# Row numbers selected with matmuls, and gathered tiles moved to dense targets 5, 9, 12, 16, 19 in a three-layer graph kernel

## The reference

```python
def _tagconv(x, src, dst, norm, W, b):          # K = 3
    out = x @ W[0]
    h = x
    for k in range(1, K + 1):
        msg = norm[:, None] * h[src]
        h = jax.ops.segment_sum(msg, dst, num_segments=x.shape[0])
        out = out + h @ W[k]
    return out + b

deg = segment_sum(ones, dst)
dis = where(deg > 0, rsqrt(maximum(deg, 1.0)), 0.0);  norm = dis[src] * dis[dst]
h = relu(_tagconv(x, src, dst, norm, W1, b1))
h = relu(_tagconv(h, src, dst, norm, W2, b2))
return layernorm(x + _tagconv(h, src, dst, norm, W3, b3))
```

## Time and profile before

| what | value |
|---|---|
| time before, median of 3 | 1302.9 us |
| the profiled execution's own time | 1303.25 us |
| its span, first to last instruction | 1301.5 us |
| TensorE busy in the span | 1249.0 us, 96% |
| GpSimd busy | 817.2 us, 63% |
| mean granted clock of TensorE | 0.994 |

### The profile page before, as it was taken

How to read it: one execution, slowest core, us unless ns; L and a number is a source line. 1 busy time by engine, 2 the same in 40 slices (tenths; PEclk the granted TensorE clock), 3 DMA queues, 4 the chain that set the end, 5 groups by cost and what they waited for, 6 DMA issues and landing times.

```text
span 1301.5 us, 19817 instructions
## 1 busy us (share of the span) xinstructions
PE 1249.0 (96%) x7584; PEld 631.7 (49%) x7584; DVE 636.8 (49%) x1621; ACT 359.5 (28%) x863; POOL 817.2 (63%) x914
## 2 busy tenths in 40 slices
PE   3789999999999999999999999999999999999996
PEld 2455555444455555444544455555444544454443
DVE  5886664344444556434443434455433433345654
ACT  3676665121112223111221112223111111112221
POOL 7347565566756572767566756573567566756673
PEclk9999999899999999999999999999999999999998
DMA  3433333344433342444354433342344344434553
GB/s 87 132 111 109 95 98 101 110 137 125 130 93 112 102 121 65 130 121 134 106 145 126 134 97 102 105 128 77 109 122 133 112 118 121 130 112 139 149 156 89
DMA packets 86967, 150.43 MB, mean 116 GB/s; under 512 B 19097, under 2 KB 60753, under 8 KB 86866
## 3 DMA queue, kind: packets, MB, share of 16 engines
q0 software_dynamic: 39184, 107.00, 29.4%
q1 hardware_dynamic: 47682, 42.10, 10.1%
HBM read 116.91 MB, written 32.11 MB: 115 GB/s over the span
## 4 chain that ended last, share of the span: by engine, by line
PE 86%; POOL 6%; issue 3%; DVE 2%; DMA 1%; ACT 1%; SPq 0%; POOLq 0%; ACTq 0%; DVEq 0%
PE pb L1093 64%; PE pb L1005 9%; POOL GB L782 4%; PE pb L1007 4%; PE pb L1024 4%; PE pb L931 2%; PE pb L1098 1%; PE pb L1071 1%; PE pb L1043 1%; DMA xr<-in_x 1%; DMA GB<-vh,KS 1%; POOL gT L696 0%; POOL g L766 0%; DVE pb L1437 0%; DVE V L1408 0%
## 5 line engine op out<-in xcount | busy, mean ns | idle before, releaser
L782 POOL DMA_INDIRECT GB<-vh,KS x810 | 779.3, 962 | 433.4 <-issue 235.5
L1093 PE MATMUL pb<-V,A 128*128 128x512 f16 x4104 | 936.7, 380 | 0.0
L1093 PEld LDWEIGHTS pb<-V,A 128*128 128x128 fp8e4 x4104 | 397.0, 98 | 442.3 <-issue 2.5
L1437 DVE SCALAR_TENSOR_TENSOR pb<-pb,cst,t 128x256 f32<-128x256 f32 (+1 forms) x225 | 110.0, 489 | 359.3 <-ACT t L896 359.2
L896 ACT ACTIVATE t<-pb,cst 128x256 f32<-128x256 f32 (+1 forms) x250 | 118.3, 473 | 500.6 <-PE pb L1098 429.3
L1005 PE MATMUL pb<-Whl,gT 128*128 128x512 f16 x576 | 204.7, 383 | 2.9 <-DVE KD L1349 1.7
L1007 PE MATMUL pb<-Whl,gT 128*128 128x256 f16 x576 | 158.0, 274 | 0.0
L1408 DVE SCALAR_TENSOR_TENSOR V<-V,pb 128x256 f16<-128x256 f16 (+1 forms) x225 | 94.1, 420 | 93.6 <-ACT V L870 93.4
L870 ACT ACTIVATE V<-pb 128x256 f16<-128x256 f32 (+1 forms) x225 | 85.7, 383 | 132.8 <-DVE pb L1437 132.7
L1005 PEld LDWEIGHTS pb<-Whl,gT 128*128 128x128 f16 x576 | 56.5, 98 | 78.7 <-issue 22.0
L1303 DVE TENSOR_REDUCE stat<-V 128x1 f32<-128x256 f16 x225 | 91.2, 411 | 0.2
(11 more groups left out here) (209 smaller groups left out, 568.6 us busy)
## 6 DMA issues: line engine op xcount, KB each, us to landing
vh<-V SPq DMA_DIRECT2D x216, 128.0 KB, 2.0
GB<-vh,KS POOLq DMA_INDIRECT x810, 2.8
xr<-in_x SPq DMA_DIRECT2D x48, 128.0 KB, 2.8
out<-g SPq DMA_DIRECT2D x24, 128.0 KB, 1.9
xr<-in_W SPq DMA_DIRECT2D x16, 128.0 KB, 2.3
V<-in_W SPq DMA_DIRECT2D x2, 512.0 KB, 4.5
vh<-V SPq DMA_DIRECT2D x18, 32.0 KB, 1.9
bb<-in_b SPq DMA_DIRECT2D x3, 128.0 KB, 5.1
```

The costliest lines, as they stand in the source:

```text
L782: pool.indirect_dma_start(GB[:, slot, :], None, vh[vbuf[(L, k + 1)]][:, :], bass.IndirectOffsetOnAxis(ap=KS[:, p:p + 1], axis=0))\
L1093: mm = pe.matmul(acc[:, :], A8[:, a, t * P:(t + 1) * P], src[:, a, :], start=False, stop=(n == NT - 1), skip_group_check=True)
L1437: dve.scalar_tensor_tensor(hi, hi, cst[0:r, 1, t:t + 1], lt, ALU.mult, ALU.add).then_inc(S["s_d1"], 1)
```

## The change

It has three parts. In the setup, `rules` becomes f32 and shrinks from twelve columns to six, `mine` holds more of the selection, and the matmuls now sum constants and selected counts in place; ACT's copy of the counts clips at zero; GpSimd needs two dependent steps for the row numbers and four for `place`. Second, `want` and `onesf` are set before that chain and not behind it. Third, `FIRST`, `STEPS`, `LATER` and the switch `hop_over` change: gathered tiles stand behind dense targets with index 4, 8, 11, 15 and 18, and the short tile 24, index 19, is the last of each hop. In hop 0 only the last two entries change (18: 22 and 19: 25 become 18: 25).

```diff
-FIRST = {3: 2, 5: 5, 7: 7, 9: 10, 11: 12, 13: 15, 15: 17, 17: 20, 18: 22, 19: 25}
-STEPS = {5: 5, 9: 10, 12: 15, 15: 20, 19: 25}
+FIRST = {3: 2, 5: 5, 7: 7, 9: 10, 11: 12, 13: 15, 15: 17, 17: 20, 18: 25}
+STEPS = {4: 5, 8: 10, 11: 15, 15: 20, 18: 25}
-RULED = 28
+RULED = 25
-LATER = (0, 2, 5, 9, 10, 15)
+LATER = (0, 0, 1, 2, 5, 9, 15)
...
-            pool.memset(rules, 0.0).then_inc(S["s_pc"], 1)
             pool.wait_ge(S["s_idx"], 1)
...
+            pool.memset(mine, 0.0).then_inc(S["s_pc"], 1)
+            pool.memset(rules, 0.0).then_inc(S["s_pc"], 1)
+            pool.memset(onesf[:, :], 1.0).then_inc(S["s_cst"], 1)
...
+            for d, a, b in ((0, 1, 1), (1, GRAN, -GRAN), (2, 1, -1), (5, -GRAN * FULL, -1)):
+                pool.memset(by[:, d, :, GV - 1], float(a)).then_inc(S["s_pc"], 1)
+                pool.memset(by[:, d, :, GV], float(b)).then_inc(S["s_pc"], 1)
...
+            picked(to[:, 0], 0, NPAIR, PW)
+            picked(to[:, 1], 2, NPAIR, PW)
+            picked(to[:, 2, :, 0:GV - 1], 0, NPAIR, GV - 1)
+            picked(to[:, 2, :, GV + 1:PW], 1, NPAIR, GV - 1)
+            picked(mine[:, 2, NE:NR].unsqueeze(2), 3, NTB, 1)
+            picked(to[:, 3, :, GV - 1:GV], 0, NPAIR, 1, -float(GRAN))
+            picked(to[:, 3, :, GV:GV + 1], 1, NPAIR, 1, float(GRAN))
...
-            pool.wait_ge(S["s_cp5"], 3)
+            pool.wait_ge(S["s_cp5"], 2)
...
-            done5(pool.tensor_scalar(vals[:, :], per[:, 12:16], 0.0, 0.0, ALU.max, ALU.add))
-            done5(pool.tensor_scalar(two[:, 0:1], vals[:, 0:1], float(FULL), 0.0, ALU.add, ALU.add))
-            done5(pool.tensor_scalar(vals[:, 2:3], vals[:, 2:3], two[:, 0:1], 0.0, ALU.min, ALU.add))
-            done5(pool.tensor_scalar(two[:, 1:2], vals[:, 0:1], per[:, 0:1], per[:, 4:5], ALU.mult, ALU.add))
...
-            done5(pool.tensor_copy(idx[0:NR, QW:QW + 1], two[:, 4:5]))
+            done5(pool.tensor_scalar(mid[:, 0:1], per[:, 4:5], float(FULL), per[:, 5:6], ALU.add, ALU.min))
+            done5(pool.tensor_scalar(idx[0:NR, QW:QW + 1], mid[:, 0:1], per[:, 0:1], per[:, 6:7], ALU.mult, ALU.add))
...
-            done5(pool.tensor_scalar(per[:, 11:12], per[:, 11:12], float(JZ), 0.0, ALU.add, ALU.add))
-            done5(pool.tensor_scalar(two[:, 5:6], vals[:, 0:1], per[:, 5:6], per[:, 9:10], ALU.mult, ALU.add))
-            done5(pool.tensor_scalar(two[:, 6:7], vals[:, 1:2], per[:, 6:7], two[:, 5:6], ALU.mult, ALU.add))
-            done5(pool.tensor_scalar(two[:, 7:8], vals[:, 2:3], per[:, 7:8], two[:, 6:7], ALU.mult, ALU.add))
+            done5(pool.tensor_scalar(mid[:, 1:2], mid[:, 0:1], per[:, 1:2], per[:, 7:8], ALU.mult, ALU.add))
...
-            pool.memset(onesf[:, :], 1.0).then_inc(S["s_cst"], 1)
...
-            act.activation(found[:, :], bank[1][0:4 * NPAIR, 0:1], ACT.Copy).then_inc(S["s_cp5"], 1)
+            act.activation(found[:, :], bank[1][0:4 * NPAIR, 0:1], ACT.Relu).then_inc(S["s_cp5"], 1)
             act.wait_ge(S["s_gc"], 2)
-            act.activation(per[:, 0:12], bank[0][0:NR, 0:12], ACT.Copy).then_inc(S["s_cp5"], 1)
-            act.wait_ge(S["s_gc"], 3)
-            act.activation(per[:, 12:16], bank[2][0:NR, 0:4], ACT.Copy).then_inc(S["s_cp5"], 1)
+            act.activation(per[:, :], bank[0][0:NR, 0:8], ACT.Copy).then_inc(S["s_cp5"], 1)
...
-            for d in range(12):
-                mm = pe.matmul(bank[0][0:NR, d:d + 1], rules[:, d, :], ones16[0:1, 0:1], start=True, stop=True,
+            pe.wait_ge(S["s_cst"], 18)
+            for d in range(4):
+                pe.matmul(bank[0][0:NR, d:d + 1], rules[:, d, :], onesf[0:1, 0:1], start=True, stop=True,
...
             for j in range(4):
-                mm = pe.matmul(bank[2][0:NR, j:j + 1], mine[:, j, :], found[:, :], start=True, stop=True,
+                mm = pe.matmul(bank[0][0:NR, 4 + j:5 + j], mine[:, j, :], found[:, :], start=True, stop=(j < 2),
+                if j >= 2:
+                    mm = pe.matmul(bank[0][0:NR, 4 + j:5 + j], rules[:, 2 + j, :], onesf[0:1, 0:1], start=False,
...
-                hop_over = (k, t) == (0, NT - 2) if k < 3 else hop_over
+                hop_over = (k, t) == (0, NT - 1) if k < 3 else hop_over
```

More of the change, by code:

```diff
@@ L484, in bass_tag_gnn_layernorm @@
         found = sb("found", [4 * NPAIR, 1], F32)
-        per = sb("per", [NR, 16], F32)
-        vals = sb("vals", [NR, 4], F32)
-        two = sb("two", [NR, 8], F32)
+        per = sb("per", [NR, 8], F32)
+        mid = sb("mid", [NR, 2], F32)
         tk = sb("tk", [P, 5, NTB], F32)
@@ L535, in bass_tag_gnn_layernorm @@
         less = gb[0:1, 256:256 + 4 * NPAIR]
-        rules = gb[0:1, 2048:2048 + 12 * NR].rearrange("p (d r) -> p d r", r=NR)
+        rules = gb[0:1, 2048:2048 + 12 * NR].bitcast(F32).rearrange("p (d r) -> p d r", r=NR)
         place = gb[0:NR, 4096:4096 + 2 * P].bitcast(F32)
@@ L704, in _ @@
-            pool.memset(by[:, 2, :, GV - 1:GV + 1], 1.0).then_inc(S["s_pc"], 1)
-            pool.memset(rules[:, 3, NE:NR], 1.0).then_inc(S["s_pc"], 1)
+            to = mine[:, :, 0:NE].rearrange("p j (u m) -> p j u m", m=PW)
+            pool.wait_ge(S["s_pc"], 6)
+            for d, a, b in ((0, 1, 1), (1, GRAN, -GRAN), (2, 1, -1), (5, -GRAN * FULL, -1)):
+                pool.memset(by[:, d, :, GV - 1], float(a)).then_inc(S["s_pc"], 1)
+                pool.memset(by[:, d, :, GV], float(b)).then_inc(S["s_pc"], 1)
@@ L711, in _ @@
[L711 to L720, removed]
@@ L721, in _ @@
-            pool.affine_select(out=mine[:, 3, NE:NR], in_=mine[:, 3, NE:NR], compare_op=ALU.not_equal, fill=1.0,
-                               base=-NPAIR * 3, pattern=[[-1, NTB]], channel_multiplier=1).then_inc(S["s_pc"], 1)
+            pool.iota(rules[:, 3, 0:NE].rearrange("p (g v) -> p g v", v=GV), pattern=[[GH, NE // GV], [0, GV]],
+                      base=ND, **iota).then_inc(S["s_pc"], 1)
+            pool.iota(rules[:, 3, NE:NR], pattern=[[GD, NTB]], base=BT * GD, **iota).then_inc(S["s_pc"], 1)
@@ new lines, in picked @@
+            def picked(z, j, n, width, value=1.0):
+                pool.affine_select(out=z, in_=z, compare_op=ALU.not_equal, fill=value, base=-NPAIR * j,
+                                   pattern=[[-1, n], [0, width]], channel_multiplier=1).then_inc(S["s_pc"], 1)
+            picked(to[:, 0], 0, NPAIR, PW)
[3 more added lines that the diff above has]
+            picked(mine[:, 2, NE:NR].unsqueeze(2), 3, NTB, 1)
@@ L723, in _ @@
+            picked(to[:, 3, :, GV - 1:GV], 0, NPAIR, 1, -float(GRAN))
+            picked(to[:, 3, :, GV:GV + 1], 1, NPAIR, 1, float(GRAN))
             pool.iota(place, pattern=[[1, P]], base=0, **iota).then_inc(S["s_pc"], 1)
+            for n, many in enumerate((float(E), 0.0, 15.0, float(E))):
+                pool.memset(want[:, n:n + 1], many).then_inc(S["s_cst"], 1)
             pool.wait_ge(S["s_pc"], RULED + 1)
-            pool.wait_ge(S["s_cp5"], 3)
+            pool.wait_ge(S["s_cp5"], 2)
@@ L755, in _ @@
             pool.tensor_tensor(wf[0:NR, P:2 * P], wf[0:NR, P:2 * P], place, ALU.add).then_inc(S["s_k5"], 1)
-            pool.memset(want[:, 0:1], float(E)).then_inc(S["s_cst"], 1)
-            pool.memset(want[:, 1:2], 0.0).then_inc(S["s_cst"], 1)
-            pool.memset(want[:, 2:3], 15.0).then_inc(S["s_cst"], 1)
-            pool.memset(want[:, 3:4], float(E)).then_inc(S["s_cst"], 1)
-            pool.memset(onesf[:, :], 1.0).then_inc(S["s_cst"], 1)
             pool.wait_ge(S["s_cs"], 1)
```

17 lines of the change are left out of this document (4 added, 13 removed).

## The result

The changed kernel took 1309.57 us, median of 5 runs (1309.05 to 1312.21), against 1302.9, the median of the five runs before (1300.92 to 1304.74): a ratio of 1.006, 95% interval 1.0048 to 1.0071. It is slower by about 0.6%; predicted were 1307.3 us and a range of 1298.5 to 1311. The spans differ by +6.1 us, and three places make that up: setup -3.4, end of hop 0 +1.6, hops 3 and 6 +8.0 (the small rest, -0.1, lies behind hop 7's first gathered tile).

The account below looks back on a forecast made before the run. TensorE is busy 1049.1 of 1050.5 us in hops 1 to 8, so the setup holds the room. 1303.25 - 4.0 + 3.4 + 5.0 = 1307.65, less 0.35 for the profiled execution: 1307.3 us, range 1298.5 to 1311.

Parts of the forecast that it names:

- Setup: Up to the first hop: a shorter GpSimd chain and an earlier `cst` save 4.0 us (bounds 1.5 and 5.5).
- each costs as much as a wide one: Setup constants on GpSimd: upper bound of +1.5 us if every narrow select costs like a wide one; +0.7 was forecast.
- The other path, `cst`: Setup on ACT: the degree root comes near 28.8 and not 33.4 us, so `cst` is ready 4.6 us earlier.
- End of hop 0: The short tile follows the gather waits instead of filling them, and the lower clock lasts longer: +3.4 us (+3.1 to +5.7).
- Hops 3 and 6: First hops of a layer: TensorE waits for deferred pieces and gathers, 2.6 us a hop at most, +5.0 for both (0 to 9).
- The other hops and the kernel's end: Hops 1, 2, 4, 5, 7, 8 and the last stores: gathers stay in time, only the last store is smaller; 0.
- the clock falls at hops 3 and 6: Rival: waits there lower the clock, 2.3 us each, and hop 0's short tile may pay as much; 1311.9 us, chance 0.09.
- the deferred pieces are absorbed: Rival: in hops 3 and 6 ACT and DVE keep up and gathers are in time; 1302.3 us, no change, chance 0.28.
- the setup gives far more: Rival: setup gives 4.6 us, projections lose half their 8.7 us idle time, hops 3 and 6 cost nothing; 1297.3 us, chance 0.13.
- hop 0's end is no longer than before: Rival: hop 0 ends no later within itself, the ring having moved, which needs gather 78 earlier; 1303.9 us, chance 0.08.

Follow-up runs that it names:

- Bank 7: The changed kernel with dense target 0 of hops 3 and 6 accumulating in PSUM bank 7, not the bank the short tile just left: 1307.09 us, ratio 1.004.
- setup only: The changed kernel with the order of before put back (`FIRST`, `STEPS`, `LATER`, `hop_over`), its setup kept: 1300.05 us, ratio 0.9977.
- short tile back: The changed kernel with `FIRST` of before alone, so hop 0's short tile again stands between the last gather matmuls: 1307.89 us, ratio 1.0036.
- constants early: The kernel before with only `want` and `onesf` set ahead of GpSimd's chain for the row numbers: 1300.15 us, ratio 0.9984.
- later demand: The setup only kernel with hop 0's gathered tiles given out one behind nearly each dense target: 1294.95 us, ratio 0.9937.

## Why the prediction was right, and which terms were off

The direction and the mechanism were right: a gain in the setup, and an order that loses more at the end of hop 0 and at hops 3 and 6. The time was 2.3 us over the forecast, inside its own range. That it came so near is in part luck: the cost of hop 0's end was set 1.8 us too high and that of hops 3 and 6 3.0 us too low.

- *Setup, -4.0 predicted, -3.4 in the trace (-2.4 by the medians).* Right in size, off in its steps. The seven selects took 2.22 us, 0.32 on average, where three had taken 0.95: the bound "each costs as much as a wide one" came nearest, and the constants came at 20.47 and not 19.6. The fetch was 0.5 us later than forecast. And behind it GpSimd's steps of 128 columns became slower, 0.97, 0.96 and two casts of 0.78 and 0.73 us, so that x was scaled from 33.17 and not 31.1. The same casts took 0.29 with only the constants moved and the steps 1.3 us later. Each stretched step lies beside DVE's one-hots (28.38 to 29.75 and 31.12 to 32.48); the step between the two, at 30.37, took 0.74 as its like did before (0.75), and in the two kernels with the old chain the one-column steps that took 0.85 and 1.25 instead of 0.34 us lie beside one-hots too. No run separates the two, so this cause is argued and not shown. The other path, `cst`, was to come 4.6 us earlier; it came 2.7 earlier, and it is what the first copy waits for. The projections behind it shifted nearly whole, by 2.7 us at that copy and 3.4 at the end of hop 0. That five memsets would do alone, the prediction did not say.
- *End of hop 0, +3.4 predicted, +1.6 in the profiled pair.* The last block came when it was forecast to, GpSimd's pace being unchanged, and the short tile did follow it. The term missed what the clock gives back. The prediction expected hop 1's first target at the lower clock still, and it ran at full clock. The low clock that before lay on 24 matmuls of hop 1 now lies partly on waiting time and on the short tile. The uncovered tile costs 3.94 us, 0.8 more than the 3.1 it took before; the first target, from its projection to the next one's, takes 5.95 us (233.58 to 239.53) and not 8.28 (233.04 to 241.32), 2.3 less, and the difference is the 1.6. In the four profiles of each kind the step is 2.7 us on average, between the two numbers.
- *Hops 3 and 6, +5.0 predicted, +8.0 in the trace.* Mis-sized, by a wait that the prediction did not have. Waits of 1.85, 0.6 and 0.8 us were forecast, and 1.84, 0.64 and 0.81 came. Target 0 of a new layer takes the bank of the short tile; before, a gathered tile of 20 matmuls lay between the two, and now the projection follows directly and waits 1.44 us for DVE's last reading of it. Bank 7 took that away and 3.1 us with it, and what is then left (403.00 - 400.82 and 402.91 - 400.11) is 5.0 us, the forecast. The prediction read `LATER` and the copies, and did not ask which buffer the moved tile holds when its successor starts.
- *The other hops and the kernel's end, 0.* As predicted, within 0.2 us: between hops 7 and 8 the first gathered tiles lie 125.77 us apart, before 125.88.
- *The rivals.* That the clock falls at hops 3 and 6 is refuted; that the short tile of hop 0 pays for it came true, with the 0.8 us above. In the stretch of hop 3 that holds the 1.84 us of waiting, 505.08 to 509.26, the granted clock was 1.00:

```profile
505.08:509.26 4.18, 2.34 (x14) 1.39 (x15) 1.97 (x6) 1.41 (x4) 0.00 (x0) 1.00 0.00 0
```

  The Trainium skill, page TensorE: Matmul & The Clock Gate, section HAM oscillation, describes waits for DMAs between bursts of matmuls that bring the clock to half. The trace of hop 0 agrees in part: the granted clock went to 0.50 among single matmuls with waits between, each of them under 1 us and shorter than those of the page's example. At hops 3 and 6 it stayed at 1.00. That the deferred pieces are absorbed is refuted by the waits; that the setup gives far more, by the projections up to 81 us, which shifted nearly whole. That hop 0's end is no longer than before did not hold either: it is 1.6 us longer in the profiled pair, 2.7 in the means.

## What to carry to other kernels

When a tile moves to the end of a stage, list what it holds (bank, buffer, queue) beside what it computes, and ask who takes it next: a bank still being read, 1.44 us at each of two layers, cost this change nearly as much as its setup won. At the end of hop 0 the waits were paid twice, once as idle time and once as the clock behind them (two single waits in hop 3 cost nothing in clock), so the demand is better moved behind the supply than the filler moved out of the gap. And before a chain of steps is rewritten, try the settings that stand in its way: five memsets of 0.09 us moved ahead of a wait gave 2.3 of the 2.4 us.

## What the runs showed of the hardware

- The low clock behind waits differs between executions of the same instructions. Behind waits of 0.5 to 0.9 us between single matmuls, 23 matmuls of hop 1 took 6.9 us (before), 7.23 (setup only), 6.43 (short tile back) and 5.33 (constants early, whose profiled execution was the fastest of its 11, 1296.58 us), and 5.13 where one wait of 0.43 us was left (later demand). In hop 3 two waits of 1.44 and 1.84 us, 4 us apart in an otherwise dense stretch, left the granted clock at 1.00.
- What a select on GpSimd over 44 partitions of f32 costs does not follow its width: 0.34 us for 110 columns and 0.28 for 44 (means of two), 0.49 for eleven that lie ten apart (the last of the seven), and 0.19 for eleven adjacent ones (the kernel before).
- On one chip of those used, TensorE paused for about 1 us before many single matmuls, above all behind hop 0 (ahead of the matmuls of dense targets alone 185 times, 195 us in sum, in the profile of the later demand), and every kernel took 33 to 35% more; the two kernels with the later demand were ahead there too, by 2%.
